# A new order of steps, a k-outer first layer and a ring of three embedding tiles in a DLRM tower on one core

## The reference

```python
e = jnp.stack([tbl_0[ids[:, 0]], ..., tbl_25[ids[:, 25]]], axis=1)      # (2048, 26, 128)
sd = jnp.einsum('bfd,bd->bf', e, dense)
ss = jnp.einsum('bfd,bgd->bfg', e, e)
z = jnp.concatenate([dense, sd, ss[:, iu, ju]], axis=1)                 # pairs i < j
h = jnp.concatenate([z, dense], axis=1)                                 # (2048, 607)
h = jnp.maximum(h @ W_top1 + b_top1, 0.0)                               # 607 x 512
h = jnp.maximum(h @ W_top2 + b_top2, 0.0)                               # 512 x 256
y = h @ W_top3                                                          # 256 x 1
```

## Time and profile before

| | |
|---|---|
| median of three runs | 405.61 us |
| the profiled execution | 404.94 us |
| its span | 403.1 us |
| PE (TensorE matmul) busy | 337.3 us, 84% |
| POOL (GpSimd) busy | 277.5 us, 69% |
| DVE (VectorE) busy | 234.1 us, 58% |
| ACT (ScalarE) busy | 204.8 us, 51% |
| mean granted TensorE clock | 0.949 of full |

### The profile page before, as it was taken

How to read it: one execution, slowest core, us unless ns; L and a number is a source line. 1 busy time by engine, 2 the same in 40 slices (tenths; PEclk the granted TensorE clock), 3 DMA queues, 4 the chain that set the end, 5 groups by cost and what they waited for, 6 DMA issues and landing times.

```text
span 403.1 us, 14210 instructions
## 1 busy us (share of the span) xinstructions
PE 337.3 (84%) x6216; PEld 301.7 (75%) x6216; DVE 234.1 (58%) x702; ACT 204.8 (51%) x289; POOL 277.5 (69%) x295
## 2 busy tenths in 40 slices
PE   0556889898989889897989899896998989898585
PEld 0545679797878769795979779683987979796384
DVE  0969968682776438680867457670587538640321
ACT  2372545566466534666465553754346654565132
POOL 6777777777777777777777777777777777773000
PEclk9998989999999989999998999998899999899559
DMA  6998233222323214223323325122141323111000
GB/s 166 246 260 261 77 84 96 79 76 83 98 81 78 76 54 110 68 80 81 96 80 79 81 57 121 55 81 78 55 122 54 99 62 81 55 52 36 3 2 1
DMA packets 19118, 35.33 MB, mean 88 GB/s; under 512 B 7168, under 2 KB 8712, under 8 KB 19056
## 3 DMA queue, kind: packets, MB, share of 16 engines
q0 software_dynamic: 9216, 18.89, 17.8%
q1 hardware_dynamic: 9824, 15.52, 13.9%
q10 hardware_dynamic: 16, 0.01, 0.0%
HBM read 34.39 MB, written 0.01 MB: 85 GB/s over the span
## 4 chain that ended last, share of the span: by engine, by line
PE 55%; POOL 12%; ACT 11%; DMA 9%; issue 8%; DVE 3%; SPq 1%; POOLq 0%
PE et_ps L565 23%; POOL rows L290 12%; PE m_ps L525 10%; PE g_ps L486 8%; ACT et L371 8%; PE m_ps L536 6%; PE et_ps L555 5%; DMA et<-tbl_in 5%; DMA rows<-tbl_in,idx 3%; ACT zt_hi L346 2%; PE m_ps L545 2%; DMA idb<-ids_one_hot 1%; DVE one_hot L406 1%; DVE zt_lo L449 1%; DVE z L442 1%
## 5 line engine op out<-in xcount | busy, mean ns | idle before, releaser
L290 POOL DMA_INDIRECT rows<-tbl_in,idx x288 | 276.7, 961 | 89.3 <-issue 84.8
L406 DVE TENSOR_SCALAR one_hot<-idb,first_row 125x256 fp32r<-125x256 int32 x512 | 159.6, 384 | 81.5 <-PE et_ps L565 78.5
L371 ACT COPY et<-et_ps 128x384 f32<-128x384 f32 (+1 forms) x128 | 123.4, 1031 | 97.8 <-PE et_ps L565 76.7
L565 PE MATMUL et_ps<-one_hot,table_hi 125*128 125x256 f32 x512 | 132.7, 297 | 22.2 <-DVE one_hot L406 18.8
L565 PE MATMUL et_ps<-one_hot,table_lo 125*128 125x256 f32 x512 | 127.1, 286 | 0.0
L565 PEld LDWEIGHTS et_ps<-one_hot,table_hi 125*128 125x128 f32 x512 | 100.1, 195 | 29.2 <-issue 20.4
L565 PEld LDWEIGHTS et_ps<-one_hot,table_lo 125*128 125x128 f32 x512 | 100.0, 195 | 0.0
L555 PE MATMUL et_ps<-ident,rows 128*128 128x128 f32 x288 | 51.1, 291 | 16.6 <-DMA rows<-tbl_in,idx 11.9
L486 PE MATMUL g_ps<-et 128*27 128x26 f32 x4096 | 54.0, 193 | 11.4 <-issue 9.2
L486 PEld LDWEIGHTS g_ps<-et 128*27 128x27 f32 x4096 | 45.3, 106 | 23.0 <-issue 15.9
L555 PEld LDWEIGHTS et_ps<-ident,rows 128*128 128x128 f32 x288 | 32.6, 145 | 22.3 <-issue 13.1
(11 more groups left out here) (46 smaller groups left out, 284.5 us busy)
## 6 DMA issues: line engine op xcount, KB each, us to landing
idb<-ids_one_hot SPq DMA_DIRECT2D x32, 256.0 KB
rows<-tbl_in,idx POOLq DMA_INDIRECT x288
et<-tbl_in SPq DMA_DIRECT2D x7, 448.0 KB
xt<-dense_t SPq DMA_DIRECT2D x8, 128.0 KB, 3.9
z<-w_z SPq DMA_DIRECT2D x2, 256.0 KB, 5.9
et<-w SPq DMA_DIRECT2D x1, 512.0 KB, 6.9
gram<-tbl_in SPq DMA_DIRECT2D x1, 448.0 KB
et<-tbl_in SPq DMA_DIRECT2D x7, 52.0 KB
```

What stands on the lines that cost most here:

```text
L290: nc.gpsimd.indirect_dma_start(out=rows[:, r, n, :], out_offset=None, in_=tables[GATHERED[k]], in_offset=bass.IndirectOffsetOnAxis(idx[par ...
L371: nc.scalar.copy(dst, src).then_inc(et_copied, 1)
L406: last = nc.vector.tensor_scalar(one_hot[n % 2][0:KP, k, :], idb[0:KP, n // 2 % ID_RING, n % 2, :], first_row[0:KP, 0:1], float(k), ALU.su ...
L565: last = nc.tensor.matmul(ps[:, n % 2 * CH:n % 2 * CH + CH], part[0:KP, n, k, :], one_hot[n % 2][0:KP, k, :], start=k == 0 and part is tab ...
```

## The change

One list PLAN, made from PHASE, gives all engines their steps with the chunk that each step belongs to:

- The first layer is k-outer: `X0` multiplies the dense features, and `K0`, `K1`, `K2` one block of z each, for all four output blocks into two whole banks of `m_ps`. `X0` stands before `A0`, and `K0` behind `Z1`.
- The bias of the first layer is a row of `w1_z`, against a column of ones in `z`. The relu takes 512 columns in one ScalarE instruction, once per half, and VectorE makes `h_lo` from the bank itself with one SCALAR_TENSOR_TENSOR per half.
- `et` is a ring of three 128-sample tiles. `G0` to `G3` use the chunk's first tile and `G4` to `G7` the second.
- `O0` to `O3` of a chunk are done half a phase ahead, in the phase of the chunk before. There are no `B` steps: VectorE makes the build of the following `O` at every `O` (one ahead). `one_hot` is a ring of 16 single products, with a semaphore step for each.
- A tile has five row slots of 4, 4, 4, 3 and 3 tables; the ring `rows` has 6 slots (before: 8 slots of 3 tables).
- Four raw tables are staged at a time. The row indices of all later chunks are one load. The weights are split after `G3` of chunk 0, and the ids of chunk 1 are loaded behind the last weights.
- In the last chunk ScalarE packs A1 and A3 and VectorE A0 and A2.

The number of matmuls, gathers, builds and z copies is unchanged.

```diff
-SCHEDULE = [(step[0], int(step[1:])) for step in (
-    "O0 B2 G4 O1 B3 G5 T0 G6 O2 B4 G7 O3 B5 A0 T1 A1 O4 O5 A2 T2 A3 T3 Z0 Z1 T4 T5 Z2 B6 B7 L0 T6 L1 T7 "
-    "O6 O7 T8 L2 G0 T9 G1 G2 T10 G3 T11 L3").split()]
+PHASE = [(step[0], int(step[1:])) for step in (
+    "T0 G4 G5 O4 T1 G6 G7 O5 X0 T2 A0 A1 O6 T3 A2 A3 O7 Z0 Z1 K0 T4 Z2 K1 "
+    "T5 G0 G1 K2 T6 G2 G3 T7 O0 T8 O1 M0 O2 T9 O3 Y0").split()]
+AHEAD = 4
+def later(kind, n):
+    if kind == "O" and n < AHEAD:
+        return 1
+    return -1 if kind in "AZXKMY" or kind == "G" and n >= G_STEPS // 2 else 0
+PLAN = [(kind, p + later(kind, n), n) for p in range(-1, NCH + 1) for kind, n in PHASE
+        if 0 <= p + later(kind, n) < NCH]
+SIZES = (4, 4, 4, 3, 3)
+OH_RING = 16
-ROW_RING = 8
+ROW_RING = 6
...
             sp.dma_start(w3s[:, :], w3).then_inc(w_in, 16)
-            sp.wait_ge(table_lo_done, 3)
-            sp.dma_start(w1_again, w1_dense[D:, :]).then_inc(w_in, 16)
+            sp.wait_ge(table_lo_done, NO)
             sp.dma_start(w2_raw.rearrange("p (k n) -> p k n", n=H2), w2.rearrange("(k p) n -> p k n", p=128))\
                 .then_inc(w_in, 16)
+            sp.dma_start(w1_again, w1_dense[D:, :]).then_inc(w_in, 16)
+            sp.dma_start(w1_raw[KZ], w1_z[(KZ - 1) * 128:, :]).then_inc(w_in, 16)
+            for pair in range(NO // 2, NCH * PAIRS):
+                load_ids(pair)
...
         def _(dve):
+            for kind, c, n in PLAN:
+                if kind == "O" and c * NO + n + 1 < NCH * NO:
+                    build(c * NO + n + 1)
+                if kind == "G" and c == 0 and n == G_STEPS // 2 - 1:
+                    split_weights()
...
         def _(pe):
+            def first_layer(c, k):
+                for m in range(4):
+                    for a, b in ((0, 0), (1, 0), (0, 1)):
+                        rhs = zt_parts[b][:, k - 1, :] if k else x_parts[b][:, :]
...
+                if kind == "O":
+                    for k in range(KT):
+                        at = (c * NO + n) * KT + k
+                        pe.wait_ge(oh_ready, at + 1)
...
+                if kind == "K":
+                    wait_a(c, A_BANKS + n)
+                    first_layer(c, n + 1)
```

More of the change, by code:

```diff
@@ L97, in z_inputs, with a_use, rows_use @@
     return rows + [-1] * (ZW - len(rows))
+def a_use(c, i):
+    use = c * A_USES + i
+    return use % 2, use // 2 + 1
+def rows_use(c, n):
+    i = c * TR_SLOTS + n
+    landed = sum(16 * SIZES[j % TR_HALF] for j in range(i % ROW_RING, i + 1, ROW_RING))
+    return i % ROW_RING, landed
 def wait(eng, sem, value):
@@ L194, in apart, with et_tile @@
             eng.sem_inc(waits_apart, 1)
[L196 to L212, removed]
+        def et_tile(tile):
+            return et[:, tile % ET_TILES * TILE_W:(tile % ET_TILES + 1) * TILE_W]
@@ L214, in _, with by_act @@
+        def by_act(c, n):
+            return c == NCH - 1 and n % 2 == 1
         @block.sync
         def _(sp):
[L216 to L228, removed]
@@ L373, in _ @@
-            phases(act, phase)
+                        act.wait_ge(w_ready, W_READY)
+                    act.wait_ge(xt_in[c % 2], (c // 2 + 1) * 16)
+                    for t in range(TILES):
+                        last = nc.scalar.copy(et_fields(TILES * c + t, F, 1)[:, 0, :],
+                                              xt[c % 2][:, t * 128:(t + 1) * 128])
+                    last.then_inc(xt_copied, 1)
+                if kind == "O" and ends_pair(n):
+                    act.wait_ge(oh_used, (c * NO + n + 1) * KT)
+                    held = n % 2 + 1
+                    src = et_ps[SLOT["O", c, n - n % 2] % 2][:, 0:held * CH]\
+                        .rearrange("d (f t b) -> d t f b", f=held, t=TILES)
+                    for t in range(TILES):
+                        last = nc.scalar.copy(et_fields(TILES * c + t, NG + n - n % 2, held), src[:, t])
+                    last.then_inc(et_copied, 1)
@@ new lines, in _ @@
+                if kind == "G" and n % 2 == 1:
+                    bank = n // 2
+                    act.wait_ge(g_done, c * G_BANKS + bank + 1)
+                    if c == 0 and n == 1:
+                        act.wait_ge(table_lo_done, NO)
+                    dst = gram[:, :].rearrange("p (f g) -> p g f", f=F)[:, bank * G_GROUPS:(bank + 1) * G_GROUPS, :]
+                    src = g_ps[bank % 2][:, 0:G_GROUPS * F].rearrange("p (g f) -> p g f", f=F)
+                    nc.scalar.copy(dst, src).then_inc(g_copied, 1)
@@ new lines, in _ @@
+                if kind == "K" and n == KZ - 1:
+                    if c == 0:
+                        act.wait_ge(w_in, W_LOADS)
+                    wait(act, h2_sums, c)
+                    for half in range(2):
+                        act.wait_ge(h1_sums, 2 * c + half + 1)
+                        nc.scalar.activation(h1_parts[0][:, 2 * half:2 * half + 2, :],
+                                             m_ps[half][:, :].rearrange("p (m b) -> p m b", m=2), ACT.Relu)\
+                            .then_inc(h1_hi_done, 1)
@@ new lines, in _ @@
+                if kind == "M":
+                    act.wait_ge(h2_sums, c + 1)
+                    wait(act, y_out, c * 16)
+                    for m in range(2):
+                        last = nc.scalar.activation(h2[:, m, :], m_ps[0][:, m * CH:(m + 1) * CH], ACT.Relu,
+                                                    bias=b2s[:, m:m + 1])
+                    last.then_inc(h2_done, 1)
+                if kind == "Y":
+                    act.wait_ge(y_sums, c + 1)
+                    nc.scalar.copy(y, m_ps[1][0:1, 0:CH]).then_inc(y_copied, 1)
+                    act.wait_ge(y_copied, c + 1)
+                    act.dma_start(out[:, c * CH:(c + 1) * CH], y).then_inc(y_out, 16)
@@ L377, in _ @@
         def _(dve):
-            dve.sem_inc(a_free, 2)
             for bank in g_ps:
```

550 lines of the change are left out of this document (261 added, 289 removed).

## The result

The changed kernel took 409.51 us (median of four runs, 408.04 to 410.83) against 404.26 us for the kernel before (four runs, 402.60 to 405.91): ratio 1.0129, 95% interval 1.0065 to 1.0193, so slower by a little over 1%. The profiled execution took 409.38 us with a span of 407.5 us. A second set of four runs (after_again) gave a ratio of 1.0154 (1.0085 to 1.0224). One of the seven runs of the kernel before that stand beside this second set took 513.01 us at a granted clock of 0.57; it says nothing of the change.

A forecast was written before the change was run, and what follows sets the result against it. The prediction took GpSimd's gathers to bound the kernel before, TensorE next, and the change to make TensorE the bound. Start, seven phases P and end gave 87.2 + 7P, with P = 46.6 413.4 us; range 401 to 420 us.

The forecast's parts named there:

- The wait ahead of K0: TensorE's wait for VectorE's copies, two builds and zt_lo: about 2.4 us, part of 3.5 us standing still per phase.
- The start: Up to T0 of chunk 1: VectorE's builds and weight split set it, 65.8 us against 61.98 before.
- The phase: TensorE's time per chunk, P: 43.2 - 1.7 + 3.5 + 0.8 = 45.8 us, 46.6 with the clock, between 45.0 and 47.5.
- The term for waits on et_ps: Three places per phase where a T needs a bank ScalarE has just emptied: 0.8 us together.
- The clock's: Slow TensorE stretch after idling, in every second phase: 0.8 us a phase, bounds 0 and 1.7.
- The end: From G4 of the last chunk to the end: 30.0 us against 31.9 before, so -1.9.
- Gathers keep their number: Under what changes nothing: gathers, matmuls, builds and z copies keep their number, with no cost added.
- of its own signs the first: Sign of being right: POOL waits for PE or ends with its last gather long before T9.
- (1): Gathers still bound it if TensorE's phase is 45.0 us or less; only the end changes: 403.0 us; chance 0.20.
- (2): On top of (1), X0 keeps the clock full over the end: another -4, about 399 us; chance 0.14.
- (3): Every phase at the lower clock or a later start, P above 47.5: 420 us and more; chance 0.09.
- (4): The 1.0 us stop inside each phase's gram products goes: P 45.6, 406.4 us; 0.1 of the forecast case's chance.

The follow-up runs named there:

- after_again: Changed kernel measured once more without an edit: 408.36 us, ratio 1.0154 to the kernel before.
- e4_before_builds_between: Kernel before, with its builds B6 and B7 moved behind A1 and A3, ahead of zt_lo: 425.47 us, ratio 1.0514.
- e5_after_fewer: Changed kernel with 74 of its 288 gathers left out (stale rows used): 405.04 us, ratio 1.0004 to the kernel before.
- e6_before_fewer: Kernel before with 88 of its 288 gathers left out (stale rows used): 394.30 us, ratio 0.9747.
- e3_first: Changed kernel with only the build of O7 moved to X0, ahead of the packing of A0: 401.04 us, ratio 0.9926 to the kernel before.
- e1_both: Changed kernel with the build of O7 moved to X0 and that of the next O0 behind the last zt_lo: 399.36 us, ratio 0.9881.
- e2_second: Changed kernel with only the build of the next O0 moved behind the last zt_lo: 405.11 us, ratio 1.0014 to the kernel before.
- e8_last: e1_both with, in the last phase only, M0 put before T8 and Y0 before T9: 398.25 us, ratio 0.9863 to the kernel before.
- e7_paced: Changed kernel with VectorE waiting for its own last instruction before a build's third, fifth and seventh comparison: 420.27 us, ratio 1.0393 to the kernel before.
- e10_last_fewer: e8_last with 74 gathers left out (stale rows used): 393.75 us, ratio 0.9698 to the kernel before.
- e9_unpaired: Changed kernel with the paired gram steps taken apart on all engines: 412.93 us, ratio 1.0250 to the kernel before.
- e1_again: e1_both measured again as reference on the same chip as e8_last: 400.31 us, ratio 0.9896 to the kernel before.

## Why the prediction was right

**The mechanism.** The forecast said that VectorE's builds in the z chain would make TensorE the bound. That is what happened: the chain of work that ended last is 64% TensorE's and 25% VectorE's and holds no gather, two builds in that place made the kernel before 5% slower with TensorE 19 us behind the gathers (e4_before_builds_between), and with some gathers left out of both, the changed kernel is 11 us slower than the kernel before (e5_after_fewer, e6_before_fewer). The wait ahead of K0 was put at 2.4 us and is 2.0 to 2.35 in the six chunks that have both builds in the chain, 2.2 in the mean; that ahead of Z0 was put at 1 and is 0.86.

**The size of the change.** The forecast was 413.4 us and the changed kernel took 409.5. The ratio is clear of 1, so "slower" is right; but the prediction laid its band for "no change", 401.5 to 409.7 us, around the 405.61 us of three runs, and 409.51 lies just inside it. By four runs the kernel before took 404.26 us.

**The start** was put at 65.8 us for T0 of chunk 1 and is at 65.67, and in after_again at 64.87. VectorE's splitting began at 47.08 us and ended at 54.83, within 1.6 us of the 48.7 and 56.3 of the working. In other executions with the same start T0 stands at 62.96 to 67.31 us, so an agreement to 0.1 us is luck.

**The phase** was put at 46.6 us and is 46.28, by two errors that nearly cancel. The term for waits on et_ps was too large: 0.8 us a phase, measured 0.3. The clock's was too small: I counted on a slow stretch in every second phase for 0.8 us, and there is one behind K0's wait in every phase. In the phase from 118.84 us the waits are 4.7 us instead of 2.7 and the busy time 41.68 instead of 40.06: 43.16 + 2.0 + 1.6 = 46.8, and the stretch is 46.73. Over the five steady phases from 118.84 us to 349.96 the busy time lies 0.8 to 2.3 us above the 40.06, so the bound of 1.7 us that the prediction gave for the clock was the better value.

**The end** was mis-sized: from G4 to the end 30.0 us forecast, 28.1 measured (379.44 to 407.5), before 31.9. X0 came out as sized, 2.61 us for 1.05 (+1.6). From A0 to K0 it took 6.1 us instead of 8.0, so -1.9 where the packing and K0 were given -1.2. From K0 to the end 14.3 us instead of 16.7, -2.4 for -2.2. The gram run, which had no term, was 1.1 shorter, with a stop of 2.33 instead of 2.73 us. Put together, 407.5 of span is 65.67 + 6 x 46.28 + 34.2 to T9 + 1.9 to G4 + 28.1. Against the 413.4 us the phases give -2.2, the way to T9 -0.4, G4 +0.5 and the end -1.9, which is the 4.0 us between forecast and profiled run.

**What was taken as unchanged and was not.** "Gathers keep their number" was right, but the prediction put their cost at nothing new, and that step was wrong: the same two builds that delay TensorE also lengthened six gathers, and the stream ended 6.9 us later. It did not show in the result because two bounds came to lie almost at the same place. In the three versions with the same last phase that the gathers bound (e3_first, e1_both, e2_second) T9 stands 3.6, 3.8 and 4.0 us behind the last gather; with the changed kernel's last gather at 373.42 us that makes 377.0 to 377.4 us for T9, an estimate, and TensorE reached it by its own path at 377.52 us. A TensorE without the waits for VectorE, beside the same gathers, would have gained next to nothing. That the forecast came out right without this term is luck, and of its own signs the first, a last gather "long before T9", was met by 4.1 us only.

**The rivals.** (1) The gathers still bound it: refuted as the prediction meant it, since TensorE has no wait for rows and its phase is 46.3 us; but lengthened gathers stand right behind, and the gathers are the bound as soon as the builds move (e1_both, e2_second, e8_last). (2) Full clock over the end: the products of X0 take 0.41 us until 386.8 us, so no. (3) More than 420 us: of the changed kernel only e7_paced came there, with longer builds; GpSimd did not stop in the changed kernel. (4) The stops inside the gram products go: in part. Three of the six phases have one of 1.0 to 1.2 us, the other three have none, and 3.7 us more stand at the start and the end of the kernel. The Trainium skill has, in "Runtime: NRT & Kernel Launch", section "Instruction fetch mechanics", instruction fetch hidden by the issue time; no run here shows whether the stops are fetches.

## What to carry to other kernels

An engine with 57% busy time can set the pace: what counts is what stands between a producer's result and its consumer in that engine's own order. Put work that nobody waits for into that engine's idle time (VectorE had 6.6 us just ahead of the chain), not between the links. Price a wait of 2 us or more on TensorE with the slow stretch behind it, here 0.8 to 2.3 us of busy time on top per phase. When the bound has moved, leave gathers out of both kernels: it shows how much of a floor they are, here 10 us in one kernel and 4.5 in the other. And when a moved instruction can touch two engines, time each one's stream after the change: the wait on one path can hide that a second path has grown to the same length.

## What the runs showed of the hardware

VectorE's comparisons and GpSimd's indirect DMAs disturb each other. With GpSimd idle a build takes 2.20 us, as in e10_last_fewer, where GpSimd's gathers (under the dots) leave the time from 235.73 to 239.66 us free:
```profile
236.97 2.20 DVE L416 TENSOR_SCALAR one_hot<-idb,first_row 125x256 fp32r<-125x256 int32 x8 [2.12 <-PE et_ps L511]
...
234.79 0.94 POOL L305 DMA_INDIRECT rows<-tbl_in,idx  x1 [0.30 <-issue]
239.66 0.99 POOL L305 DMA_INDIRECT rows<-tbl_in,idx  x1 [3.94 <-PE et_ps L503]
```
Beside gathers it mostly takes 2.3 to 2.6 us and the gathers 0.94. In some places VectorE is not slowed: the build takes 2.17 to 2.19 us, and the gather stands until the build is over and ends 0.1 or 0.8 us behind it, after 1.9 to 2.9 us in all. Behind the start the changed kernel falls into this six times and after_again as well, e5_after_fewer thirteen times, e9_unpaired five times, e2_second four times, e4_before_builds_between twice, e3_first once, and the kernel before, e1_both, e1_again, e6_before_fewer, e7_paced, e8_last and e10_last_fewer never. The Trainium skill, "SBUF — State Buffer", section "Who interferes with whom", says that a tensor_scalar can take the port pair that VectorE shares with GpSimd for a whole instruction, with GpSimd blocked meanwhile, if its operands allow a mode that uses both ports. The trace agrees in that the gathers stand; that the shared ports are the reason, and which mode these comparisons ran in, no run shows. The gathers stood for eight instructions on end and not for one, and three short pauses in the build (e7_paced) put an end to it. Which order of starts leads into it is open.
